# One-hot matrices of the gated layer: eight two-operation instructions a group in place of two wide ones

## The reference, cut to what matters

```
h = max(layernorm(x), 0)
edge_input = concat([h[src], edge_attr_32])            # 100000 x 128
messages = gelu(edge_input @ mW1 + mb1) @ mW2 + mb2
gates = sigmoid(gelu(edge_input @ gW1 + gb1) @ gW2 + gb2)     # one number per edge
aggregated = segment_sum(messages * gates, dst)        # 3125 x 96
update = gelu(concat([h, aggregated]) @ uW1 + ub1) @ uW2 + ub2
x = x + layernorm(h + update) * ln_g + ln_b
```

## Time and profile before

| | |
|---|---|
| median of 3 runs | 3176.62 us |
| the profiled execution's own time | 3170.49 us |
| its span, first to last instruction | 3168.8 us |
| busy in the span | PE 84%, PEld 70%, DVE 75%, ACT 20%, POOL 38% |
| mean granted TensorE clock | 0.939 |
| gated layer, steady turns | about 2300 to 3090 us of the span |
| all 99 L1568 and all 99 L1570 | 68.5 us and 68.7 us busy |

### The profile page before, as it was taken

The page is one execution under the profiler, slowest core; times in us unless marked ns, Lnnn a source line. Parts: engine busy times, 40 slices in busy tenths (PEclk is TensorE's granted clock), DMA queues, the critical chain, the costliest instruction groups (busy, mean ns, idle before and its releaser), DMA issues.

```text
span 3168.8 us, 72113 instructions
## 1 busy us (share of the span) xinstructions
PE 2675.9 (84%) x25058; PEld 2208.0 (70%) x25059; DVE 2367.4 (75%) x6307; ACT 640.5 (20%) x1255; POOL 1206.4 (38%) x1205
## 2 busy tenths in 40 slices
PE   4677777889999997996999999997689888888884
PEld 1222222789999997995999999997567677666663
DVE  7888877853332356448888888887799999999986
ACT  0011222510000005011111111111233333333331
POOL 0000000000000000003777777773477777777771
PEclk9999999899999998997999999998799999999996
DMA  1000000000000000003544444441333333333330
GB/s 30 0 0 0 0 0 0 2 1 2 2 1 2 2 2 5 2 1 81 130 120 117 119 116 117 119 115 38 95 103 107 102 107 108 104 104 109 102 98 19
DMA packets 108153, 180.74 MB, mean 57 GB/s; under 512 B 36346, under 2 KB 69900, under 8 KB 107867
## 3 DMA queue, kind: packets, MB, share of 16 engines
q0 software_dynamic: 47824, 89.19, 11.4%
q1 hardware_dynamic: 60043, 87.59, 9.8%
HBM read 171.88 MB, written 4.80 MB: 56 GB/s over the span
## 4 chain that ended last, share of the span: by engine, by line
POOL 34%; issue 11%; DVE 5%; PE 2%; DMA 1%; ACT 0%; DVEq 0%; POOLq 0%; ACTq 0%
POOL gate_rows L1417 20%; POOL msg_rows L1046 14%; DVE pre_space L1120 2%; PE msg_sums L1242 1%; DMA first_rows<-pre_space 0%; DVE msg_rows L1144 0%; DVE pre_space L1540 0%; PE gate_sums L1671 0%; DMA msg_rows<-h_rows,all_src_i 0%; PE msg_sums L1257 0%; ACT msg_src_near L1058 0%; DMA msg_src_row<-src_rows 0%; DVE pre_space L1212 0%; DVE msg_rows L1140 0%; DVE msg_t L1199 0%
## 5 line engine op out<-in xcount | busy, mean ns | idle before, releaser
L1417 POOL DMA_INDIRECT gate_rows<-first_rows,all_src_i x637 | 648.8, 1019 | 198.3 <-issue 193.8
L1046 POOL DMA_INDIRECT msg_rows<-h_rows,all_src_i x539 | 535.6, 994 | 164.1 <-issue 163.8
L1242 PE MATMUL msg_sums<-pre_parts,pre_space 125*128 125x192 f16 x6125 | 531.2, 248 | 37.8 <-DVE pre_space L1120 37.7
L1033 POOL MEMSET pre_middle<- 125x1 f32 x1 | 0.1, 99 | 1465.7 <-POOLq L677 1465.7
L605 PE MATMUL hop_sums<-dense_work,dense_counts 125*128 125x192 f16 (+1 forms) x6250 | 531.7, 247 | 20.5 <-DVE dense_work L569 8.2
L605 PEld LDWEIGHTS hop_sums<-dense_work,dense_counts 125*128 125x128 f16 x6250 | 528.6, 98 | 23.6 <-DVE dense_work L569 10.0
L1242 PEld LDWEIGHTS msg_sums<-pre_parts,pre_space 125*128 125x128 f16 x6125 | 512.3, 99 | 44.8 <-DVE pre_space L1120 39.2
L1646 PE MATMUL gate_sums<-pre_space,pre_parts 125*96 125x384 f16 x2450 | 448.1, 343 | 5.5 <-DVE pre_parts L1514 5.5
L439 PE MATMUL cnt_sums<-cnt_hot,cnt_near 128*128 x1000 | 338.9, 407 | 109.9 <-DVE cnt_hot L371 109.3
L1120 DVE TENSOR_SCALAR pre_space<-msg_src_near,pre_node_no 125x640 f16<-125x640 f16 x1225 | 393.4, 394 | 11.5 <-ACT msg_src_near L1058 11.4
L1646 PEld LDWEIGHTS gate_sums<-pre_space,pre_parts 125*96 125x96 f16 x2450 | 309.2, 129 | 133.0 <-issue 28.8
(11 more groups left out here) (276 smaller groups left out, 3163.5 us busy)
## 6 DMA issues: line engine op xcount, KB each, us to landing
msg_edge<-edges SPq DMA_DIRECT2D x98, 384.0 KB
msg_src_row<-src_rows SPq DMA_DIRECT2D x49, 312.5 KB
gate_edge<-edges SPq DMA_DIRECT2D x98, 128.0 KB
gate_rows<-first_rows,all_src_i POOLq DMA_INDIRECT x637
gate_src_row<-on_src SPq DMA_DIRECT2D x49, 187.5 KB
msg_rows<-h_rows,all_src_i POOLq DMA_INDIRECT x539
gate_inputs<-on_edges SPq DMA_DIRECT2D x49, 48.0 KB, 2.2
first_rows<-pre_space SPq DMA_DIRECT2D x6, 375.0 KB
```

Source lines behind the costliest of these rows:

```text
L1046: nc.gpsimd.indirect_dma_start(out=rows[:, r, k, :], out_offset=None, in_=table, in_offset=bass.IndirectOffsetOnAxis(ap=src_i[:, at:at + 1 ...
L1242: last = nc.tensor.matmul(got[group % 2][:, n, 0:2 * D], pick[:, c % 2, j, i * EP:(i + 1) * EP], parts[:, j, :], start=(j == 0), stop=(j = ...
L1417: nc.gpsimd.indirect_dma_start(out=rows[:, r, k, :], out_offset=None, in_=table, in_offset=bass.IndirectOffsetOnAxis(ap=src_i[:, at:at + 1 ...
```

## The change

L1568 and L1570 become eight `tensor_scalar` instructions per step, one for each edge tile: each compares 64 node numbers with a per-partition number (the edge's target) and multiplies by a second per-partition number (the edge's gate). Both numbers are read from memory by address (a [128, 1] operand each). The "+ 1" moves to ScalarE, a second instruction per group over the same 8 numbers, which waits for the Tanh (`gate_turned`) and counts up `gate_out` in its place. The semaphore `onehot_made` and the wait for it are gone.

```
                 act.wait_ge(gate_sum, group + 1)
                 nc.scalar.activation(gate[:, group % 3, :], gate[:, group % 3, :], ACT.Tanh, scale=0.5,
-                                     bias=gb2_sb[:, 0:1]).then_inc(gate_out, 1)
+                                     bias=gb2_sb[:, 0:1]).then_inc(gate_turned, 1)
+                act.wait_ge(gate_turned, group + 1)
+                nc.scalar.activation(gate[:, group % 3, :], gate[:, group % 3, :], ACT.Copy,
+                                     bias=1.0).then_inc(gate_out, 1)
...
-                    nodes = iota[:, bass.ds(at, SPAN)].unsqueeze(1).to_broadcast([EP, GT, SPAN])
-                    targets = dst_f[:, group * GT:(group + 1) * GT].unsqueeze(2).to_broadcast([EP, GT, SPAN])
-                    open_by = gate[:, group % 3, :].unsqueeze(2).to_broadcast([EP, GT, SPAN])
-                    hot = onehot[:, slot, :, :]
-                    nc.vector.tensor_tensor(hot, nodes, targets, ALU.is_equal).then_inc(onehot_made, 1)
-                    dve.wait_ge(onehot_made, step + 1)
-                    nc.vector.scalar_tensor_tensor(out=hot, in0=open_by, scalar=1.0, in1=hot,
-                                                   op0=ALU.add, op1=ALU.mult).then_inc(onehot_ready, 1)
+                    nodes = iota[:, bass.ds(at, SPAN)]
+                    for k in range(GT):
+                        target = dst_f[:, group * GT + k:group * GT + k + 1]
+                        last = nc.vector.tensor_scalar(onehot[:, slot, k, :], nodes, target,
+                                                       gate[:, group % 3, k:k + 1], ALU.is_equal, ALU.mult)
+                    last.then_inc(onehot_ready, 1)
```

More of the change, by code:

```diff
@@ L1360, in gated_layer @@
         gate_out = m.sem("gate_out"); group_done = m.sem("group_done")
-        onehot_made = m.sem("onehot_made"); onehot_ready = m.sem("onehot_ready")
+        gate_turned = m.sem("gate_turned"); onehot_ready = m.sem("onehot_ready")
         step_summed = m.sem("step_summed"); step_added = m.sem("step_added"); all_summed = m.sem("all_summed")
```

## The result

The changed kernel took 3345.32 us (median of 4 runs, 3331.87 to 3350.29) against 3177.26 for the kernel before (median of 4). The measured ratio is 1.0512, with a 95% interval from 1.0492 to 1.0532; the quotient of the two medians is a little higher, 1.0529. The kernel is slower, as forecast, but by 168 us where 46 were forecast, and outside the range.

A forecast was written before the change was run, and what follows sets the result against it. VectorE was taken to set the pace, with GpSimd close behind. Spacing +42.6, collisions +12 and vanished waits -9 gave +45.6 us on 3176.6, so 3222 us, with an 8-in-10 range of 3173 to 3251.

The forecast's parts named there:

- The spacing of the eight: Eight instructions on VectorE, 0.221 us apart, take 1.77 us against 1.34 a step: +42.6 us over 99 steps.
- the upper of the two bounds: Second number from memory in each of VectorE's eight instructions: 0 to 61 ns, taken as 61.
- VectorE's collisions under the eight, +12: GpSimd's gathers slow VectorE's eight by 7%, as they do the picks: +12 us, bounds 0 and 25.
- ScalarE, 0: ScalarE's extra instruction takes 0.2 to 0.4 us a turn, but the gates have a turn to spare: 0.
- The end, 0 ± 4: GpSimd's two wide additions at the end come earlier, at another VectorE instruction, at a similar price: 0, +-4 us.
- GpSimd is relieved ... with VectorE slower it has time to spare in any case: GpSimd loses the collisions with L1568 and L1570, pays for the eight, and has time to spare at 6.5 gathers a turn.
- the -9: VectorE's waits for gathered rows, 9.2 us in all, go because GpSimd gets ahead: -9 us.
- VectorE sets the pace: In the gated layer's steady turns VectorE, busy 730.8 of 790 us, bounds; GpSimd follows within a small margin.
- the rivals' sums: Dearer eight, 8 x 0.255: 3250 us, chance 0.10; numbers fetched early, 8 x 0.10, GpSimd pacing: 3157 us, chance 0.06.

The follow-up runs named there:

- the broken picks: Changed kernel with a sum over 8 numbers after each third pick: 3239.99 us, ratio 1.0210 to the kernel before.
- the four sums: Changed kernel with four small sums of 8 elements between the eight and the picks: 3234.82 us, ratio 1.0174 to the kernel before.
- changed kernel, picks first: Changed kernel with the picks ahead of the eight in each turn, nothing else: 3172.77 us, ratio 0.9982 to the kernel before.
- ScalarE multiplies: VectorE keeps only the wide comparison, ScalarE multiplies by the gates in eight products a step: 3150.14 us, ratio 0.9926 to the kernel before.
- the run with the gate's stream: Changed kernel with the gate as a second SBUF input stream of the eight, not a number from memory: 3260.86 us, ratio 1.0280 to the kernel before.
- one small sum: Changed kernel with one small sum of 8 elements between the eight and the picks: 3318.63 us, ratio 1.0458 to the kernel before.

## Why the prediction was wrong

- **The spacing of the eight: right.** 0.223 us against 0.221 forecast, and 44 us against 42.6. The second number costs 60 ns, the upper of the two bounds and the value taken. For VectorE this agrees with what the Trainium skill ("ScalarE: Activation LUTs", section "What ACT_TABLE_LOAD costs") says for ScalarE, that each such operand adds its own share.
- **VectorE's collisions under the eight, +12: too much.** Eight and their successor start 1.78, 1.79 and 1.82 us apart in the rows shown, against 8 x 0.223 = 1.78 undisturbed.
- **ScalarE, 0: right,** by the run with its part alone. **The end, 0 ± 4:** it came out at +2.7; the wide additions now stop the eight, as the timeline of the end shows, where they stopped L1540.

```profile
3259.39 12.81 DVE L1570 TENSOR_SCALAR gate_onehot<-pre_iota,pre_dst_f,gate_gate 128x64 f32 x8
...
3261.04 5.25 POOL L1422 TENSOR_TENSOR pre_space<-all_h,pre_ub 125x2400 f32<-125x2400 f32 x1
```

- **"GpSimd is relieved ... with VectorE slower it has time to spare in any case", and with it the -9: this step failed.** Instead of 9.2 us of waits that vanish there are 139.8. Two faults are in it. The first is one of reading: "VectorE sets the pace". The earlier trace rows already gave GpSimd 788 of 790 us, it never waits for its ring in the kernel before, and the chain that ended last runs through its gathers. So it had no time to spare, a slower VectorE gives it some only if its gathers don't lengthen, and whatever lengthens them lengthens the layer. The second is that the collision was priced for VectorE alone, with nothing for the gathers. I took the gathers at 0.95 to 1.05 us under picks as a property of picks. It holds for gathers that start well into the picks, or behind a wide instruction; in the kernel before only 4 start 0.05 to 0.25 us after the first pick. In the changed kernel 57 do, behind the eight, and 52 of them wait for up to 13 picks: 163.3 us more of gathers. The breaks show it: with the run of picks interrupted, 100 us come back.
- The Trainium skill ("SBUF — State Buffer", section "Who interferes with whom") was weighed at that place. It has a two-port instruction hold the port for its whole length. The trace goes further: not one instruction of 0.3 us is waited for but the unbroken run of them, 3.69 us for one gather. That it is this port which the held gathers lack is the page's account; the runs show only beside which instructions they are held. I had used the rule for VectorE's side of the price only.
- **Without held gathers the sum was nearly right**: 34.6 us by the broken picks, 29 by the four sums, against 45.6 forecast, or 33.6 without its collision term. These two are estimates, each a difference of two runs, and neither is the kernel that was forecast.
- Two slips in the rivals' sums change nothing: 2.04 x 7% x 99 is 14, not 13, and 8 x 0.10 is 0.80, not 0.82.

What stays open: why a gather that starts 0.05 to 0.45 us after the first pick is held. Its start alone doesn't decide. Behind L1546's sum 86 gathers start 0.05 to 0.25 us after the first pick (changed kernel, picks first) and behind the wide comparison 71 (ScalarE multiplies), and none of them is held. So what stands ahead of the picks counts too: all the versions with many held gathers have eight short instructions there, with at most two small sums in between. Whether it is their shortness, their number, or the number from memory that each of them reads (the wide ones read none) was not tested apart.

## What to carry to other kernels

Before saying that an engine has time to spare, add its busy time and its issue gaps over the stretch and compare with the stretch: two engines can be full at once, and then a collision must be priced for both. A run of eight short instructions straight ahead of a run of 12 or 13 picks let one gather be held for the whole run of picks here; another order of the same instructions was worth 174 us, and one small instruction of another kind after every third pick 100 us. A long run placed just ahead of a loop's entry hides that entry (0.33 us a turn), but whether this wins must be measured: it cost 13 us where ScalarE multiplies.

## What the runs showed of the hardware

- A held gather ends with the run of picks, not with one pick, and in two ways: 0.82 us after it in 70 of the 81 in the changed kernel (44 of 51 in the run with the gate's stream), and 0.12 us after it in most of the 77 with one small sum (2505.15 + 3.08 = 2508.23 beside picks that end at 2508.11). The 0.82 stands in the kernel before too, behind a two-input instruction: 2499.91 + 1.53 against 2499.68 + 0.95.

```profile
2505.05 3.06 DVE L1512 TENSOR_SCALAR pre_space<-gate_src_near,pre_node_no 125x384 f16<-125x384 f16 x13
...
2505.15 3.08 POOL L1418 DMA_INDIRECT gate_rows<-first_rows,all_src_i  x1 [0.30 <-issue]
```

- Behind the eight short instructions 52 of 57 gathers that start 0.05 to 0.25 us after the first pick last over 2 us; behind one wide comparison none of 71 does (1.05 us at most).
- On VectorE a second per-partition number from memory costs 60 ns an instruction, as the first does (61 by the earlier trace rows): 64 elements of f32 take 0.163 us apart with one and 0.223 with two.
- The entry into a loop with bounds from memory leaves VectorE idle for 0.33 us behind the single sum L1543, and not at all behind a run of 12 or 13 picks.
